# Ternary network of a two-layer kernel: VectorE normalises, copies and splits the next batch's rows two slots ahead of their old places

## The chip, the cores and the metric

One core of a Trainium2 chip runs the whole program. The time is device microseconds for one execution. Four compute engines work side by side, each with its own instruction stream, and wait for each other by semaphores: TensorE (PE: matmuls and transposes; its weight loads are PEld), VectorE (DVE), ScalarE (ACT) and GpSimd (POOL). SyncE (SP) issues the DMAs that store the result.

## The reference

The input is x, 16 batches of 512 rows of 256. Four parts are added to it in turn, each fed with a layer norm of x; only the last one is touched here:

```python
def _ternary_linear(x, w):
    alpha = jnp.mean(jnp.abs(w))
    w_t = jnp.sign(w) * (jnp.abs(w) > 0.5 * alpha).astype(w.dtype)
    ...
    rms = jnp.sqrt(jnp.sum(x * x, axis=-1, keepdims=True)) / jnp.sqrt(jnp.asarray(d, x.dtype))
    x_norm = x / (rms + EPS)
    return jnp.einsum('bsd,fd->bsf', x_norm, w_q)
h = jax.nn.gelu(_ternary_linear(x, w_up), approximate=False)
return _ternary_linear(h, w_down)
```

x has 256 columns, h has 1024. The weights become -1, 0 or 1; the rows are scaled by their root mean square before each of the two products. The second scale is applied at the end, to the finished product.

## The kernel before, in words

All 16 batches of x stay in SBUF. The last of the four parts is `ternary_feed_forward` (from L2180). It works one batch after the other (b = 0 to 15) and, in each, in eight slots (f = 0 to 7), one for each 128 of the 1024 hidden columns. A slot has the number n = 8b + f, so there are 128 slots. Each engine has its own hand-written loop over n, and the order of calls in a loop is the order of that engine's work.

What one slot does:

- **TensorE** (`up`, L2221, matmuls at L2230): four matmuls of 128 x 512 make the hidden columns in one of three PSUM banks. Four, because x is kept as two float32r parts, a rounded one and the rest, and has two halves of 128 columns.
- **ScalarE**: `gelu` (L2275) in place in the bank, `high_part` (L2280), the rounded copy of h, and `square` (L2292).
- **VectorE**: `low_part` (L2326), the rest of h, which is h less its rounded copy.
- **GpSimd** (L2406): adds the squares up over the eight slots of a batch, in slots 1 to 7.
- **TensorE** again, three slots later (`T_LAG`): `down` (L2234, matmuls at L2244), eight matmuls of 128 x 256 into the PSUM banks of the batch's result. In the loop of TensorE a slot is thus `up(n)`, then `down(n - 3)`.

Around it, once for each batch, stands the preparation of the next batch's rows, in two pairs of 128-row tiles:

- `normal(b + 1, pair)` (L2302, instructions at L2309) on VectorE writes two normalised tiles into `shared_xn`, a buffer for one pair.
- `turn_x(b + 1, pair)` (L2214, transposes by the helper `turn_blocks`, L120) on TensorE turns them into `prep_bank`, one PSUM bank that both pairs use in turn, after slot 1 (pair 0) and after slot 4 (pair 1). It waits for the normalised pair, and for `low_x` of the pair before, which has to have read the bank.
- `keep_x` (L2316) on VectorE copies the bank out as the rounded part, and `low_x` (L2320) writes the rest. Both read `prep_bank`, so `keep_x` waits for `turn_x` of its own pair.

The last part is the end of a batch. After slot 7 TensorE adds the squares over the partitions (`row_sums`, L2255, of the batch before). Then come `hidden_mean` on VectorE, `hidden_root` on GpSimd (L2395), and in slot 0 of the batch after that `hidden_scale` on VectorE (L2336, L2338). `finish(b - 2, t)` (L2344) multiplies a tile of the product out of PSUM by its scale and adds it to x: tiles 0 and 1 in slot 0, tiles 2 and 3 in slot 1 behind that slot's `low_part`. Two pairs of PSUM banks hold the products of the batches by turns, so the first `down` of batch b, which TensorE issues in slot 3, waits for the four `finish` of batch b - 2:

```python
q.wait_ge(s["x_added"], added(b - 2) if b >= 2 else 0)
```

The other wait of this kind is in `up(n)`: it needs `low_part(n - 3)`, which has to have read the PSUM bank. The order of VectorE's work is set by the constant at L2179: `T_XN_AT` says in which slots the two `normal` stand, `T_TURN_AT` where `turn_x` stands on TensorE, `T_KEEP_AT` where `keep_x` and `low_x` stand.

Of the kernel before, what the change touches and what calls it, by code (L numbers as in the profile page):

```python
# [1709 lines left out]
FC = F // P  # L1710
# [465 lines left out]
H_BANKS = 3  # L2176


T_XN_AT, T_TURN_AT, T_KEEP_AT, T_SUMS_AT = (0, 2), (1, 4), (2, 5), 7  # L2179
def ternary_feed_forward(net, ternary, start, result):  # L2180


# [1 line left out]
    nc, B, L, D, T = net.nc, net.B, net.L, net.D, net.T  # L2184
    n_slots = B * FC
    with ExitStack() as ctx:
# [112 lines left out]
        def dve(q):  # L2299
            e = q.e  # L2300

            def normal(b, pair):  # L2302
                late = b >= FIRST_ROWS
                q.wait_ge(s["scale"], 2 if late else 0)
                q.wait_ge(s["turned"], 2 * b + pair)
                for tt in range(2):
                    t = b * T + 2 * pair + tt
                    by = scale[:, t - start.rows:t - start.rows + 1] if late else start.scale[:, t:t + 1]
                    i = e.tensor_scalar(xn[:, tt, :], net.x[:, t, :], net.mean_var[:, t, 0:1], by,  # L2309
                                        ALU.subtract, ALU.mult)  # L2310
                i.then_inc(s["xn"])

            def keep_x(b, pair):
                q.wait_ge(s["turned"], 2 * b + pair + 1)
                q.wait_ge(s["up"], (b - 1) * FC)
                e.tensor_copy(x_part(b, pair, 0), prep_bank[:, :].rearrange("p (c t) -> p c t", c=2)).then_inc(s["x_hi"])  # L2316

            def low_x(b, pair):
                q.wait_ge(s["x_hi"], 2 * b + pair + 1)
                e.tensor_tensor(x_part(b, pair, 1), prep_bank[:, :].rearrange("p (c t) -> p c t", c=2), x_part(b, pair, 0),  # L2320
                                ALU.subtract).then_inc(s["x_lo"])

            def low_part(n):
                q.wait_ge(s["h_hi"], n + 1)
                q.wait_ge(s["h_squared"], n + 1)
                e.tensor_tensor(h_parts[:, n % H_BUFS, 1, :], h_banks[n % H_BANKS][:, :], h_parts[:, n % H_BUFS, 0, :],  # L2326
                                ALU.subtract).then_inc(s["h_lo"])

            def hidden_mean(b):
                q.wait_ge(s["h_rows"], b + 1)  # L2330
                e.tensor_scalar(hs[:, b % 2, :], prep_bank[:, 0:T], 1.0 / F, None, ALU.mult).then_inc(s["h_mean"])

            def hidden_scale(b):
                out = hs[:, b % 2, :]
                q.wait_ge(s["h_rms"], b + 1)
                e.tensor_scalar(out, out, 1e-8, None, ALU.add).then_inc(s["h_rms_eps"])  # L2336
                q.wait_ge(s["h_rms_eps"], b + 1)
                e.reciprocal(out, out).then_inc(s["h_scale"])  # L2338

            def finish(b, t):  # L2340
                xs = net.x[:, b * T + t, :]
                q.wait_ge(s["h_scale"], b + 1)
                q.wait_ge(s["down"], (b + 1) * FC)
                e.scalar_tensor_tensor(out=xs, in0=down_banks[2 * (b % 2) + t // 2][:, (t % 2) * D:(t % 2 + 1) * D],  # L2344
                                       scalar=hs[:, b % 2, t:t + 1], in1=xs, op0=ALU.mult, op1=ALU.add).then_inc(s["x_added"])

            def scales():
                q.wait_ge(s["std"], 2)
                e.reciprocal(scale[:, :], scale[:, :]).then_inc(s["scale"])
                q.wait_ge(s["scale"], 1)  # L2350
                e.tensor_tensor(rms[:, :], rms[:, :], scale[:, :], ALU.mult).then_inc(s["rms"])
                q.wait_ge(s["rms"], 1)
                e.tensor_scalar(rms[:, :], rms[:, :], 1e-8, None, ALU.add).then_inc(s["rms"])
                q.wait_ge(s["rms"], 2)
                e.reciprocal(rms[:, :], rms[:, :]).then_inc(s["rms"])
                q.wait_ge(s["rms"], 3)
                e.tensor_tensor(scale[:, :], scale[:, :], rms[:, :], ALU.mult).then_inc(s["scale"])

            for f in range(FC):
                e.tensor_copy(up_w[:, :, f * P:(f + 1) * P], ternary.up[:, :, f * P:(f + 1) * P]).then_inc(s["up_wide"])  # L2360
            for n in range(n_slots + 2 * FC):
                b, f = divmod(n, FC)
                if n < n_slots:
                    low_part(n)
                if b + 1 < B and f in T_XN_AT:
                    normal(b + 1, T_XN_AT.index(f))
                if b + 1 < B and f in T_KEEP_AT:
                    keep_x(b + 1, T_KEEP_AT.index(f))
                    low_x(b + 1, T_KEEP_AT.index(f))
                if 0 < b <= B and f == T_SUMS_AT:  # L2370
                    hidden_mean(b - 1)
                if n == SCALES_AT:
                    scales()
                if 2 <= b < B + 2 and f == 0:
                    hidden_scale(b - 2)
                if 2 <= b < B + 2 and f < 2:
                    finish(b - 2, 2 * f)
                    finish(b - 2, 2 * f + 1)
# [41 lines left out]
        with nc.Block() as block:  # L2420
            @block.sync
            def _(e):
                sp(Seq(e))

            @block.scalar
            def _(e):
                act(Seq(e))

            @block.vector
            def _(e):  # L2430
                dve(Seq(e))

            @block.gpsimd
            def _(e):
                pool(Seq(e))

            @block.tensor
            def _(e):
                pe(Seq(e))
# [47 lines left out]
```

## Time and profile before

| | us |
|---|---|
| median of 3 runs | 2664.49 (2663.3 to 2668.45) |
| the profiled execution | 2662.7 |
| its span in the profile | 2660.9 |
| ternary part in the profile, from its first matmul | 2363.5 to the end |
| mean granted share of the TensorE clock | 0.986 |

The profiled execution is 1.8 us longer than its span, since a little lies around the span, and it is 1.8 us below the median of the runs. In the profile "idle before" is time in which an engine did nothing just ahead of an instruction, with the engine and line that ended the wait. The full granted clock, 1.00, is 2.4 GHz; 0.50 is 1.2 GHz. A matmul's duration runs to its modelled end, which lies behind the start of the next.

### The profile page before, as it was taken

How to read it: one execution, taken by the hardware profiler on the slowest of the kernel's cores; microseconds unless marked ns; L12 is line 12 of the kernel's file. 1: busy time of each engine (PE TensorE's matmuls, PEld its weight loads, DVE VectorE, ACT ScalarE, POOL GpSimd, SP SyncE). 2: the span in 40 equal slices, each digit the busy share in tenths (PEclk: the TensorE clock that was granted, in tenths of full speed). 3: DMA queues.
4: the chain of work that ended last, by engine and by line, in shares of the span. 5: the costliest groups of instructions: out<-in, count | busy, mean ns of one | idle time of the engine just before them, and what ended most of it. 6: DMA issues, size and time to landing. Idle time of an engine off the chain costs nothing. (4 is left out here: it accounts for less than half of the span.)

```text
span 2660.9 us, 73392 instructions
## 1 busy us (share of the span) xinstructions
PE 2514.8 (95%) x26276; PEld 1807.2 (68%) x26276; DVE 2135.9 (80%) x6793; ACT 2003.7 (75%) x3679; POOL 1693.0 (64%) x3088
## 2 busy tenths in 40 slices
PE   5999999999999999999879999999999999989998
PEld 3677777777777777777523336777777776768887
DVE  5999999999989999998674667888888888746665
ACT  4998999998899998998624447766676667657776
POOL 3767667667667767767451227777776777756555
PEclk8999999999999999999989999999999999999999
DMA  4334234334234434425100126566566556400001
GB/s 124 64 67 83 56 67 84 72 58 84 62 60 84 79 57 78 73 48 86 36 8 1 36 51 115 96 104 106 93 102 104 103 97 98 71 2 25 33 33 40
DMA packets 110378, 182.09 MB, mean 68 GB/s; under 512 B 27008, under 2 KB 96384, under 8 KB 97920
## 3 DMA queue, kind: packets, MB, share of 16 engines
q1 hardware_dynamic: 106176, 175.82, 35.5%
q8 instruction: 211, 3.46, 0.6%
q10 hardware_dynamic: 3840, 1.58, 0.3%
q14 instruction: 151, 1.24, 0.2%
HBM read 116.25 MB, written 60.29 MB: 66 GB/s over the span
## 5 line engine op out<-in xcount | busy, mean ns | idle before, releaser
L923 POOL TENSOR_TENSOR ratio_scores<-ratio_scores,ratio_max_cols 128x512 f32<-128x512 f32 (+3 forms) x1024 | 727.7, 728 | 318.3 <-DVE ratio_max_cols L808 312.5
L199 PE MATMUL bank<-ratio_k_stack,ratio_q_stack 102*128 102x512 bf16 (+7 forms) x2048 | 506.0, 303 | 33.6 <-DVE ratio_max_cols L808 17.5
L1483 DVE CUSTOM_DVE_ANT_0 zeroed_unused<-bank,zeroed_drop 128x512 bf16<-128x512 f32 (+3 forms) x1024 | 439.7, 484 | 107.3 <-PE bank L199 107.2
L808 DVE CUSTOM_DVE_ANT_0 ratio_scores<-bank,ratio_scores 128x512 f32<-128x512 f32 (+3 forms) x1024 | 472.5, 490 | 22.2
L1365 ACT ACTIVATE arena<-bank 128x512 f32<-128x512 f32 x640 | 370.3, 593 | 150.8 <-PE bank L1258 149.4
L657 ACT ACTIVATE ratio_prob<-bank 128x512 f32<-128x512 f32 x640 | 378.7, 592 | 104.9 <-PE bank L555 102.4
L798 DVE TENSOR_TENSOR ratio_scores<-bank,ratio_inverse 128x512 f32<-128x512 f32 x640 | 436.2, 682 | 16.8 <-PE bank L199 9.6
L552 PE MATMUL bank<-const_f_sb,ratio_scores 128*128 128x128 f32 x2560 | 410.0, 274 | 0.9 <-ACT ratio_prob L657 0.9
L646 ACT ACTIVATE ratio_inverse<-bank 128x512 f32<-128x512 f32 x640 | 381.1, 596 | 12.5 <-PE bank L202 12.5
L650 ACT ACTIVATE ratio_inverse<-ratio_inverse 128x1024 f32<-128x1024 f32 x320 | 338.7, 1058 | 10.1
L1617 POOL TENSOR_SCALAR_AFFINE_SELECT arena<-arena 128x256 f32<-128x256 f32 (+1 forms) x640 | 229.1, 364 | 163.7 <-ACT arena L1365 159.8
L552 PEld LDWEIGHTS bank<-const_f_sb,ratio_scores 128*128 128x128 f32 x2560 | 301.5, 141 | 42.3 <-issue 2.0
L199 PEld LDWEIGHTS bank<-ratio_k_stack,ratio_q_stack 96*128 96x128 bf16 (+1 forms) x2048 | 179.0, 98 | 193.4 <-DVE ratio_max_cols L808 109.3
L1258 PE MATMUL bank<-zeroed_q_stack,zeroed_k_stack 99*128 99x128 bf16 x2560 | 249.7, 219 | 11.7 <-ACT arena L1365 10.6
L199 PE MATMUL bank<-zeroed_k_stack,zeroed_q_stack 96*128 96x512 bf16 (+3 forms) x1024 | 248.0, 305 | 2.8 <-PEq L2153 2.1
L1258 PEld LDWEIGHTS bank<-zeroed_q_stack,zeroed_k_stack 99*128 99x128 bf16 x2560 | 178.2, 97 | 91.5 <-ACT arena L1365 55.5
L2406 POOL TENSOR_TENSOR ternary_square_sum<-ternary_square_sum,ternary_squares 128x512 f32<-128x512 f32 x112 | 144.8, 1293 | 121.3 <-ACT ternary_squares L2292 120.9
L555 PE MATMUL bank<-const_b_sb 128*128 128x128 bf16 x1024 | 211.9, 219 | 0.0
L202 PE MATMUL bank<-const_b_sb 128*128 128x128 bf16 x1024 | 193.1, 220 | 0.0
L1951 ACT ACTIVATE lowrank_hidden<-bank,lowrank_b 128x512 f32<-128x512 f32 x128 | 82.2, 684 | 133.5 <-PE bank L1833 133.4
L214 PE MATMUL bank<-arena,zeroed_v_ones 128*32 128x128 f32 x5120 | 179.4, 276 | 0.9
L214 PE MATMUL bank<-ratio_prob,ratio_v_ones 128*32 128x128 f32 x5120 | 179.4, 276 | 0.0
(219 smaller groups left out, 4973.6 us busy)
## 6 DMA issues: line engine op xcount, KB each, us to landing
ratio_q_stack<-ratio_parts_q SPq DMA_DIRECT2D x186, 128.0 KB
ratio_k_stack<-ratio_parts_k SPq DMA_DIRECT2D x186, 128.0 KB
zeroed_q_stack<-zeroed_parts_q SPq DMA_DIRECT2D x186, 128.0 KB, 4.4
zeroed_k_stack<-zeroed_parts_k SPq DMA_DIRECT2D x186, 128.0 KB, 7.5
ratio_parts_q<-arena SPq DMA_DIRECT2D x96, 128.0 KB
ratio_parts_k<-arena SPq DMA_DIRECT2D x96, 128.0 KB
zeroed_parts_q<-shared_parts SPq DMA_DIRECT2D x96, 128.0 KB
zeroed_parts_k<-shared_parts SPq DMA_DIRECT2D x96, 128.0 KB
```

The costliest lines, as they stand in the source:

```text
L199: i = e.matmul(bank[:, off:off + w], qs[0:rows, s, hh, ib * P:(ib + 1) * P], ks[0:rows, s, hh, 0:w], start=(k == 0), stop=mask is None, sk ...
L214: i = e.matmul(o_bank[32 * h:32 * h + 32, ib * P:(ib + 1) * P], values_ones[:, vs, jb, (g % 2) * GROUP + h, :], prob[:, (base + u) % bufs, ...
L552: e.matmul(bank[:, at], scores[:, n % S_BUFS, at], net.ident, is_transpose=True, start=first, stop=False, skip_group_check=True)
L646: e.activation(inv[:, n % INV_BUFS, :], shared("denoms", n)[:, :], ACT.Ln, scale=-2.0, bias=EPS_RATIO).then_inc(s["log_den"])
L650: e.activation(both, both, ACT.Exp, scale=-1.0).then_inc(s["inverse"])
L657: e.activation(prob[:, n % PROB_BUFS, 0:wd], exp_banks[n % 2][:, 0:wd], ACT.Exp).then_inc(s["prob"])
L798: e.tensor_tensor(scores[:, n % S_BUFS, 0:wd], dot_banks[n % 2][:, 0:wd], inv[:, n % INV_BUFS, 0:wd], ALU.mult).then_inc(s["weighed"])
L808: i = e.tensor_tensor_reduce(seg, dot_banks[n % 2][:, at], seg, 1.0, 0.0, ALU.mult, ALU.max, mx[:, pair % M_BUFS, c:c + 1])
L923: i = e.tensor_tensor(seg, seg, mx[:, pair % M_BUFS, c:c + 1].to_broadcast([P, w]), ALU.subtract)
L1258: i = e.matmul(bank[:, off + jb * P:off + (jb + 1) * P], ks[0:STACK + FOLD_ROWS, st, hh, jb * P:(jb + 1) * P], qs[0:STACK + FOLD_ROWS, st, ...
L1365: e.activation(prob[:, n % FOLD_PROBS, 0:wd], exp_banks[n % 2][:, 0:wd], ACT.Exp, scale=0.25).then_inc(s["prob"])
L1483: i = e.tensor_tensor_reduce(unused[:, n % 2, at], bank[:, at], drop[:, L - (ib + 1) * P:L], 1.0, 0.0, ALU.add, ALU.max, mx[:, pair % FOLD ...
```

## The change

Three constants and VectorE's loop change. TensorE's loop stays as it is, with its transposes after slots 1 and 4.

```diff
-T_XN_AT, T_TURN_AT, T_KEEP_AT, T_SUMS_AT = (0, 2), (1, 4), (2, 5), 7
+T_XN_AT, T_TURN_AT, T_KEEP_AT, T_SUMS_AT = (-2, 0), (1, 4), (0, 3), 7
...
             for f in range(FC):
                 e.tensor_copy(up_w[:, :, f * P:(f + 1) * P], ternary.up[:, :, f * P:(f + 1) * P]).then_inc(s["up_wide"])
+            normal(1, 0)
             for n in range(n_slots + 2 * FC):
                 b, f = divmod(n, FC)
                 if n < n_slots:
                     low_part(n)
-                if b + 1 < B and f in T_XN_AT:
-                    normal(b + 1, T_XN_AT.index(f))
                 if b + 1 < B and f in T_KEEP_AT:
                     keep_x(b + 1, T_KEEP_AT.index(f))
                     low_x(b + 1, T_KEEP_AT.index(f))
+                if b + 1 < B and f == T_XN_AT[1]:
+                    normal(b + 1, 1)
+                if b + 2 < B and f == FC + T_XN_AT[0]:
+                    normal(b + 2, 0)
                 if 0 < b <= B and f == T_SUMS_AT:
                     hidden_mean(b - 1)
```

VectorE's order in one batch, by slot, each time behind that slot's `low_part`:

| slot | before | after |
|---|---|---|
| 0 | normal pair 0; hidden_scale; finish 0, 1 | keep_x, low_x pair 0; normal pair 1; hidden_scale; finish 0, 1 |
| 1 | finish 2, 3 | finish 2, 3 |
| 2 | normal pair 1; keep_x, low_x pair 0 | |
| 3 | | keep_x, low_x pair 1 |
| 5 | keep_x, low_x pair 1 | |
| 6 | | normal pair 0 of the batch after the next |
| 7 | hidden_mean | hidden_mean |

## Rows read from the trace of the kernel before

**Rows 1.** The page: busy time of each engine, its share of the span.

```profile
PE 2514.8 (95%) x26276; PEld 1807.2 (68%) x26276; DVE 2135.9 (80%) x6793; ACT 2003.7 (75%) x3679; POOL 1693.0 (64%) x3088
```

**Rows 2.** Busy time by stretch: stretch, length, five engines, clock, DMA share, GB/s.

```profile
2380.00:2655.00 275.00, 262.48 (x1718) 235.88 (x1716) 172.18 (x347) 202.81 (x365) 158.74 (x127) 1.00 0.08 28
```

**Rows 3.** Who waited for whom, TensorE, ternary part: us in total, times, longest.

```profile
PE bank L120 <- DVE shared_xn L2309: 7.5, 15, 1.8
PE bank L120 <- DVE ternary_x_parts L2320: 2.9, 7, 1.0
PE bank L120 <- DVE ternary_first_parts L2320: 2.5, 7, 0.4
```

**Rows 4.** Timeline of TensorE, batch 5, slots 1 to 4: start, us, what.

```profile
2457.15 1.11 PE L2244 MATMUL bank<-ternary_down_wide,ternary_h_parts 128*128 128x256 f32 x8
2458.67 0.66 PE L120 MATMUL bank<-const_f_sb,shared_xn 128*128 128x128 f32 x4 [0.41 <-DVE shared_xn L2309]
2459.08 1.17 PE L2230 MATMUL bank<-ternary_x_parts,ternary_up_wide 128*128 128x512 f32 x4
...
2461.04 1.09 PE L2230 MATMUL bank<-ternary_x_parts,ternary_up_wide 128*128 128x512 f32 x4
2461.97 1.11 PE L2244 MATMUL bank<-ternary_down_wide,ternary_h_parts 128*128 128x256 f32 x8
...
2465.30 0.63 PE L120 MATMUL bank<-const_f_sb,shared_xn 128*128 128x128 f32 x4 [0.35 <-DVE ternary_first_parts L2320]
```

**Rows 5.** Timeline of VectorE, batch 5, slots 0 to 3.

```profile
2457.89 0.73 DVE L2309 TENSOR_SCALAR shared_xn<-x,mean_var,ternary_first_scale 128x256 f32<-128x256 f32 x2
...
2459.74 0.68 DVE L2326 TENSOR_TENSOR ternary_h_parts<-bank,ternary_h_parts 128x512 fp32r<-128x512 f32 x1
2460.33 0.87 DVE L2344 SCALAR_TENSOR_TENSOR x<-bank,ternary_h_scale,x 128x256 f32<-128x256 f32 x2
...
2462.70 1.14 DVE L2309 TENSOR_SCALAR shared_xn<-x,mean_var,ternary_first_scale 128x256 f32<-128x256 f32 x2
2463.75 0.68 DVE L2316 CAST ternary_first_parts<-bank 128x512 fp32r<-128x512 f32 x1
2464.47 0.69 DVE L2320 TENSOR_TENSOR ternary_first_parts<-bank,ternary_first_parts 128x512 fp32r<-128x512 f32 x1
2465.07 1.46 DVE L2326 TENSOR_TENSOR ternary_h_parts<-bank,ternary_h_parts 128x512 fp32r<-128x512 f32 x2
```

**Rows 6.** Timeline of GpSimd, batch 5, slots 1 and 2.

```profile
2459.13 1.30 POOL L2406 TENSOR_TENSOR ternary_square_sum<-ternary_square_sum,ternary_squares 128x512 f32<-128x512 f32 x1 [2.38 <-ACT ternary_squares L2292]
2462.06 1.29 POOL L2406 TENSOR_TENSOR ternary_square_sum<-ternary_square_sum,ternary_squares 128x512 f32<-128x512 f32 x1 [1.64 <-ACT ternary_squares L2292]
```

**Rows 7.** Timeline of TensorE, batch 0, slots 1 to 3.

```profile
2368.82 0.66 PE L120 MATMUL bank<-const_f_sb,shared_xn 128*128 128x128 f32 x4 [1.81 <-DVE shared_xn L2309]
...
2370.50 1.91 PE L2230 MATMUL bank<-ternary_first_parts,ternary_up_wide 128*128 128x512 f32 x4
2372.20 0.41 PE L2244 MATMUL bank<-ternary_down_wide,ternary_h_parts 128*128 128x256 f32 x1
```

**Rows 8.** Timeline of TensorE: behind a short wait and behind two long ones.

```profile
57.60 0.39 PE L199 MATMUL bank<-ratio_k_stack,ratio_q_stack 96*128 96x256 bf16 x2 [1.29 <-DVE ratio_max_cols L808]
...
1314.13 0.70 PE L1833 MATMUL bank<-arena 64*128 64x512 f32 x2 [2.13 <-PEq L1007]
...
2324.60 0.23 PE L1266 MATMUL bank<-const_b_sb,zeroed_m_parts 128*128 128x128 bf16 x1 [1.83 <-POOL zeroed_m_parts L1609]
```

**Rows 9.** Busy time by stretch: after three long waits of TensorE, and around a short one.

```profile
1315.22:1318.63 3.41, 3.39 (x12) 1.11 (x10) 1.17 (x3) 3.27 (x5) 0.06 (x1) 0.50 0.71 211
...
2325.56:2328.97 3.41, 3.17 (x19) 2.67 (x17) 2.86 (x12) 1.61 (x6) 3.08 (x12) 0.50 0.02 4
2369.94:2373.35 3.41, 3.41 (x13) 2.83 (x12) 0.81 (x2) 2.54 (x5) 1.20 (x2) 0.50 0.00 0
57.00:62.50 5.50, 4.68 (x42) 4.01 (x43) 5.40 (x18) 4.13 (x7) 4.31 (x7) 1.00 1.09 170
```

## The prediction, made before the changed kernel was run

> **What bounds the kernel now.** I read the page first: TensorE is busy for 95% of the span [rows 1]. The change touches only the ternary part, so I then read the busy time by stretch for it: from 2380 to 2655 us TensorE is busy for 262.5 of 275 us at the full clock, while VectorE has 172 us of work [rows 2]. TensorE bounds this part, and a change pays or costs by what it does to TensorE's waits. The view of waits names them: 7.5 us before transposes for `normal`, and 2.9 + 2.5 us before transposes for `low_x`, 12.9 us in all, over 15 batches that prepare a next one [rows 3]. These are the waits the change moves work away from. VectorE has room on average, so the question is only which of its results comes late inside a batch.
>
> The timelines of batch 5 give the steady pattern. Every batch's `down` in slot 1 is followed by a wait of 0.41 us, then the transposes; those of pair 1 wait 0.35 us [rows 4]. A matmul group's modelled end lies 0.16 us behind the next group's start where nothing waits (2461.04 + 1.09 against 2461.97 [rows 4]), and this overlap is lost at a wait. So the two waits cost 0.57 + 0.51 = 1.08 us per batch.
>
> **What is removed.** After the change `normal` of pair 0 is made in slot 6 of the batch before, and `low_x` of pair 0 ends in slot 0 or 1, long before TensorE reaches slot 4. Both waits go: 1.08 us in each of batches 1 to 14. No instruction is added or removed, and no DMA is issued elsewhere in the order, except that the store of a batch's result waits for `finish`; it is off the path until the last batches, where the order is unchanged.
>
> **What is added.** `keep_x` of pair 0 now stands in slot 0 of VectorE and waits for transposes that TensorE issues at the end of slot 1. Behind it in VectorE's queue stand `low_x`, `normal` of pair 1, `hidden_scale`, `finish` 0 and 1, `low_part` of slot 1 and `finish` 2 and 3. For the last two somebody waits: the first `down` of the batch, in slot 3, needs all four `finish`. I walk through batch 5, with slots 0 to 3 as n = 40 to 43.
>
> 1. TensorE, nothing waited for: `down(38)` starts at 2457.15 and the transposes follow 0.94 later (the spacing of 2461.04 to 2461.97), at 2458.09; today 2458.67 [rows 4]. Everything behind moves up by 0.58 as well: `down(40)` could start at 2461.39 in place of 2461.97.
> 2. The transposes take 0.63 [rows 4]; VectorE starts some 0.04 later, at 2458.76 (I estimate this handover from the 0.05 between the end of `normal`, 2458.62, and the transposes, 2458.67 [rows 4, 5]).
> 3. `keep_x` to `low_x` is 0.72, `low_x` to the next instruction 0.60 [rows 5]: `normal` of pair 1 starts at 2460.08.
> 4. GpSimd's addition of slot 1 runs from 2459.13 to 2460.43 [rows 6]. Today the pair that starts at 2462.70 beside the addition of 2462.06 to 2463.35 takes 1.14 us and ends 0.49 behind it; with GpSimd idle a pair takes 0.73 [rows 5, 6]. So I let the pair end at 2460.43 + 0.49 = 2460.92, not at 2460.81.
> 5. From the end of the pair of `normal` to the start of `low_part` is 1.12 (2458.62 to 2459.74, with `hidden_scale` and `finish` 0 and 1 between); from there to `finish` 2 and 3 is 0.59, and these take 0.87 [rows 5]. They end at 2463.50. TensorE can start `down(40)` at 2463.55.
>
> That is 2.16 us after 2461.39, of which about 2.0 will show as idle time. Of the 2.16 us, 1.08 is paid for by the two waits removed: **net +1.08 us per batch**. It falls on the batches that both prepare a next one and finish an old one, b = 2 to 14, 13 batches: +14.0 us. The bounds of the stall: without the GpSimd collision and with immediate handovers it is 2.0; with a whole addition of 1.30 waited for [rows 6] in place of 0.11 it is 3.3. I take 2.16, as the addition's end is known from the same timeline.
>
> `up(44)` in slot 4 needs `low_part(41)`, which ends at 2462.7 in this walk, before `down(40)`; so this does not add a second wait. `low_part` of slot 4 comes some 1.5 us later than today and nobody needs it before slot 7. In slot 6 `normal` stands where VectorE waits for ScalarE anyway.
>
> **Step 4 by rule.** The trace shows the longer pair beside GpSimd's addition [rows 5, 6]. The Trainium skill, page "SBUF — State Buffer", section "SBUF: two separate sides", says that VectorE and GpSimd share one pair of ports as an exclusive lock and that the one that starts first holds it for the whole instruction. By that rule the pair waits for the addition's end, as in step 4; without it the 13 stalls would sum to 1.4 us less.
>
> **The first batches.** Batch 1 has no `finish` in it and only gains, 1.1 us. Batch 0 waits 1.81 us today before its first transposes, and later runs at half clock: `up(3)` to `down(0)` takes 1.70 us there (2370.50 to 2372.20) [rows 7], against 0.93. With `normal(1, 0)` ahead of the loop the wait of 1.81 + 0.16 = 1.97 us can go, and the half-clock stretch of 2369.94 to 2373.35 [rows 9] with it (1.53 us, worked out below): 3.5 us at most. But `low_part(1)`, which `up(4)` needs, then stands behind `keep_x`, `low_x` and the pair of `normal`, 0.72 + 0.60 + 1.14 = 2.5 us of work [rows 5], of which some 1 us will show. I take 2.3 us, between 0.5 (the half-clock stretch stays and the 1 us shows) and 3.5. Sum so far: 14.0 - 1.1 - 2.3 = **+10.6 us**.
>
> **The clock.** New waits of 2.0 us are as long as those behind which the clock fell. The waits that ended at 1314.13 (2.13 us), at 2324.60 (1.83 us) and at 2368.82 (1.81 us) [rows 7, 8] were each followed, some 1 us after their end, by a stretch of 3.41 us at 1.2 GHz [rows 9]; behind a wait of 1.29 us, which ended at 57.60 [rows 8], the clock stayed at 2.4 GHz [rows 9]. In such a stretch two groups of 1.70 us find room that take 0.94 each at full clock: 3.41 - 1.88 = 1.53 us lost. If all 13 stalls are followed by one: 13 x 1.53 = **+19.9 us**. The likeliest sum is 10.6 + 19.9 = +30.5 us. Against the profiled execution's 2662.7 that is 2693.2; the median of the runs shown lies 1.8 higher, so I forecast 2695.
>
> The Trainium skill speaks against this term: the page "TensorE: Matmul & The Clock Gate", section "HAM oscillation — how this bites in real kernels", warns only of idle gaps longer than any in this walk. By that page the clock would stay up. The rows speak the other way, three of three, but it is a rival below.
>
> **Rivals.**
> - *The stall comes and the clock holds.* For it: each wait stands alone in a batch of otherwise unbroken matmuls. Against: the wait of 1.83 us had matmuls on both sides too. The time is 2664.5 + 10.6 = 2675. A mix is possible: with 8 of 13 stalls followed by a slow stretch it is 2687.
> - *Faster.* The place is `down` of slot 3 and its wait for `finish` 2 and 3. If VectorE had them done by 2461.39 in batch 5's terms, nothing would be late and each batch would gain its 1.08: 14 x 1.08 + 2.3 = 17.4 us less, 2647. It decides at a stall of 1.08 us; above that the batch loses. My chain ends 2.16 late, and every link of it is a row, so the chain would have to be a whole microsecond shorter. That could be only if `keep_x` were not held by the transposes; but it reads what they write.
> - *No change in effect:* the removed waits come back as waits of about 1.1 us, for `finish` or for `low_part`, 2664 give or take 4. This needs a chain 1.1 us shorter, too.
>
> **Chances.** Stall with most stalls followed by slow clock (2685 to 2702): 0.66. Stall without, or with few: 0.24. Faster: 0.05. Even: 0.05. A measurement of this kernel can tell about 0.2%, 5.3 us, from no change; both stall cases lie above it. The range of 8 in 10 reaches from the clock-holding case, 2674, to the forecast plus a stall 0.5 us longer in 13 batches, 2702. All in all faster 0.05, same 0.05, slower 0.90.
>
> **What would show it.** In the waits of the changed kernel the transposes' waits for L2309 and L2320 should be gone but for batch 0, and a new line should stand there: TensorE, L2244, waiting for `finish` (L2344), 13 times, some 26 us in total, 2.0 each. VectorE should show some 1 us idle before `keep_x` of pair 0, released by the transposes. Of the clock, stretches of 3.4 us at 0.50 should follow the stalls, and the distance from batch to batch should grow by 1.1 us without and by 2.6 us with one. The forecast is wrong if the new wait is under 1.1 us or absent, or if the granted clock stays at 1.00 throughout.

## The result, and the profile after

The changed kernel takes 2694.77 us (median of 6 runs, 2687.2 to 2698.14) against 2665.69 for the kernel before in as many runs. The ratio is 1.0102 with a 95% interval of 1.0083 to 1.0121: slower by 29 us. The forecast was 2695, range 2674 to 2702.

The view of waits, TensorE, ternary part of the changed kernel (us in total, times, longest), against [rows 3]:

```profile
PE bank L2244 <- DVE x L2344: 27.5, 13, 2.1
PE bank L120 <- DVE shared_xn L2309: 1.4, 1, 1.4
```

The 29 waits of the transposes, 12.9 us in all, are gone but for the first one. In their place stand 13 waits of the first `down` of a batch for `finish`. To see why that wait is 2.1 us long, read VectorE's timeline of batch 5 from the top, slots 0 to 2 (compare [rows 5]):

```profile
2456.14 0.69 DVE L2326 TENSOR_TENSOR ternary_h_parts<-bank,ternary_h_parts 128x512 fp32r<-128x512 f32 x1 [2.02 <-ACT ternary_square_sum L2292]
2457.59 0.69 DVE L2316 CAST ternary_first_parts<-bank 128x512 fp32r<-128x512 f32 x1 [0.76 <-PE bank L120]
2458.32 0.69 DVE L2320 TENSOR_TENSOR ternary_first_parts<-bank,ternary_first_parts 128x512 fp32r<-128x512 f32 x1
2458.93 0.83 DVE L2309 TENSOR_SCALAR shared_xn<-x,mean_var,ternary_first_scale 128x256 f32<-128x256 f32 x2
...
2460.87 0.68 DVE L2326 TENSOR_TENSOR ternary_h_parts<-bank,ternary_h_parts 128x512 fp32r<-128x512 f32 x1
2461.47 0.87 DVE L2344 SCALAR_TENSOR_TENSOR x<-bank,ternary_h_scale,x 128x256 f32<-128x256 f32 x2
```

and TensorE's of the same stretch (compare [rows 4]):

```profile
2456.01 1.11 PE L2244 MATMUL bank<-ternary_down_wide,ternary_h_parts 128*128 128x256 f32 x8
2456.95 0.60 PE L120 MATMUL bank<-const_f_sb,shared_xn 128*128 128x128 f32 x4
2457.31 1.17 PE L2230 MATMUL bank<-ternary_x_parts,ternary_up_wide 128*128 128x512 f32 x4
2458.31 1.10 PE L2244 MATMUL bank<-ternary_down_wide,ternary_h_parts 128*128 128x256 f32 x8
2459.25 1.09 PE L2230 MATMUL bank<-ternary_x_parts,ternary_up_wide 128*128 128x512 f32 x4
2462.48 1.88 PE L2244 MATMUL bank<-ternary_down_wide,ternary_h_parts 128*128 128x256 f32 x8 [2.14 <-DVE x L2344]
2464.16 1.91 PE L2230 MATMUL bank<-ternary_x_parts,ternary_up_wide 128*128 128x512 f32 x4
```

The transposes follow the `down` 0.94 us later and wait for nothing. VectorE stands idle 0.76 us before `keep_x`, and the two last `finish` end at 2462.34. TensorE starts `down` at 2462.48, 2.14 us idle. What follows is the second half of the loss: this `down` takes 1.68 us to the start of the next `up` and not 1.02, as the one of 2524.41 does behind its wait, for the clock has fallen. Busy time by stretch, with the clock as the third number from the end, behind two of the waits and behind a third:

```profile
2421.70:2425.11 3.41, 3.41 (x14) 3.02 (x14) 0.45 (x1) 0.69 (x2) 0.35 (x1) 0.50 0.45 154
2442.18:2445.59 3.41, 3.41 (x14) 3.02 (x13) 0.64 (x2) 0.38 (x1) 0.56 (x1) 0.50 0.46 156
2524.41:2527.82 3.41, 3.41 (x25) 3.24 (x26) 1.05 (x2) 1.24 (x3) 0.98 (x1) 1.00 0.46 154
```

At 0.50 the same 3.41 us hold 14 matmuls, at 1.00 they hold 25. The DMA engines were as busy in the third as in the other two (0.46, 0.45, 0.46), so their traffic doesn't set the slow stretches apart. In the profiled execution 11 of the 13 waits were followed by one; the first, of 2.03 us, and the seventh, whose end is at 2524.41, were not. The price of one can be read from the starts of `low_part` of slot 0 in batches 8, 9 and 10:

```profile
2518.06 0.69 DVE L2326 TENSOR_TENSOR ternary_h_parts<-bank,ternary_h_parts 128x512 fp32r<-128x512 f32 x1 [2.00 <-ACT ternary_square_sum L2292]
...
2537.25 0.69 DVE L2326 TENSOR_TENSOR ternary_h_parts<-bank,ternary_h_parts 128x512 fp32r<-128x512 f32 x1 [2.02 <-ACT ternary_square_sum L2292]
...
2557.91 0.69 DVE L2326 TENSOR_TENSOR ternary_h_parts<-bank,ternary_h_parts 128x512 fp32r<-128x512 f32 x1 [2.00 <-ACT ternary_square_sum L2292]
```

Batch 8, with a wait and no slow stretch, is 19.19 us long; batch 9, with both, is 20.66. The kernel before needs 17.92 to 17.99.

The books of the two profiled executions: from the first `up` to the end of the span it was 297.4 us before (2363.5 to 2660.9) and is 324.7 now (2360.8 to 2685.5), +27.3. The whole spans differ by 24.6 only, because the work ahead of the ternary part, the same in both, happened to end 2.7 us earlier (in the twelve profiles of this document the first `up` starts anywhere from 2359.9 to 2366.3). This profiled execution is among the quick ones of its kernel (2687.2, the others 2688.61 to 2698.14), so it has less than the whole 29 us in it.

### The profile page after: what moved, and what is told of

It is laid out like the page before. It is cut to its first block and busy times, and to the rows that moved or that the text cites. A ratio compares the mean times of both kernels' runs of the same rounds, so it can differ in the third digit from the quotient of the medians.

```text
span 2685.5 us, 73406 instructions
## 1 busy us (share of the span) xinstructions
PE 2522.7 (94%) x26276; PEld 1815.8 (68%) x26276; DVE 2137.3 (80%) x6793; ACT 2003.5 (75%) x3679; POOL 1688.2 (63%) x3088
## 3 DMA queue, kind: packets, MB, share of 16 engines
q10 hardware_dynamic: 3840, 1.58, 0.4%
```

## Experiments

All times are medians, and each is compared with the kernel before on the same chip in the same hours, whose median was 2662.96, 2664.7 and 2666.53 us in the three sets. In the first set are the finish first, eight matmuls in the wait, `normal` behind and `normal` only; in the last one matmul in the wait and GpSimd's wait; the rest in the second. The sets ran on different chips, and the changed kernel (2694.77 against 2665.69) belongs to none of them. So a difference between kernels of two sets is known only to some 3 us.

### The finish first

```diff
-T_XN_AT, T_TURN_AT, T_KEEP_AT, T_SUMS_AT = (-2, 0), (1, 4), (0, 3), 7
+T_XN_AT, T_TURN_AT, T_KEEP_AT, T_SUMS_AT = (-2, 1), (1, 4), (1, 3), 7
...
                 if 2 <= b < B + 2 and f < 2:
                     finish(b - 2, 2 * f)
                     finish(b - 2, 2 * f + 1)
+                if b + 1 < B and f == T_KEEP_AT[0]:
+                    keep_x(b + 1, 0)
+                    low_x(b + 1, 0)
+                    normal(b + 1, 1)
```

> The changed kernel, but keep_x and low_x of pair 0 and normal of pair 1 stand in slot 1 behind finish 2 and 3, not in slot 0 ahead of them. Theory (the four finish are late for the first down of a batch, and the clock falls behind each such wait): the wait of L2244 for L2344 is gone, no slow stretch is left in the ternary part, the waits of the transposes stay gone, and the time is some 17 us below the kernel before, 2648 to 2650 by its median of 2665.7. Rival one (making keep_x wait for transposes on VectorE is itself what costs): a wait of TensorE for low_part or for normal takes the place, time at 2665 or above. Rival two (the slower clock has another cause in this part): slow stretches remain, time 2655 to 2668.

Measured: 2645.8 us, ratio 0.993 (0.9917 to 0.9942). Behind the first matmuls of the ternary part the view of waits has one line for TensorE, and the clock holds over the steady batches (busy time by stretch):

```profile
PE bank L120 <- DVE shared_xn L2309: 0.2, 1, 0.2
```

```profile
2400.00:2640.00 240.00, 234.51 (x1566) 214.75 (x1564) 169.20 (x327) 184.07 (x331) 144.22 (x115) 1.00 0.10 35
```

The timelines of TensorE and VectorE in one batch show what is different:

```profile
2467.33 0.60 PE L120 MATMUL bank<-const_f_sb,shared_xn 128*128 128x128 f32 x4
...
2470.59 1.12 PE L2244 MATMUL bank<-ternary_down_wide,ternary_h_parts 128*128 128x256 f32 x8
```

```profile
2467.52 0.87 DVE L2344 SCALAR_TENSOR_TENSOR x<-bank,ternary_h_scale,x 128x256 f32<-128x256 f32 x2
2468.38 0.69 DVE L2326 TENSOR_TENSOR ternary_h_parts<-bank,ternary_h_parts 128x512 fp32r<-128x512 f32 x1
2468.99 0.87 DVE L2344 SCALAR_TENSOR_TENSOR x<-bank,ternary_h_scale,x 128x256 f32<-128x256 f32 x2
2469.77 0.68 DVE L2316 CAST ternary_x_parts<-bank 128x512 fp32r<-128x512 f32 x1
2470.49 0.69 DVE L2320 TENSOR_TENSOR ternary_x_parts<-bank,ternary_x_parts 128x512 fp32r<-128x512 f32 x1
```

VectorE does not stand idle for the transposes, which end at 2467.93: it starts the first `finish` at 2467.52 and has the last done at 2469.86, 0.73 us before the first `down` of the batch starts at 2470.59. `keep_x` then finds its bank full and does not wait. So neither the copies nor their being early cost anything; their place ahead of `finish` did. This version is 17 us faster than the kernel before. It is 49 us faster than the changed kernel by the medians, and 46 if each is taken against its own kernel before. Rival one and rival two of the expectation are out.

### Work in the wait

Eight matmuls of 128x512 that nobody needs, ahead of the first `down` of batches 2 to 14 of the changed kernel:

```diff
+            def fill(b):
+                q.wait_ge(s["x_lo"], 2 * (b + 1) + 1)
+                for k in range(FILL):
+                    e.matmul(prep_bank[:, :], up_w[:, 0, 0:P], x_parts[b % 2][:, 0, 0, :], start=True, stop=True)
...
                 if n < n_slots:
                     up(n)
+                if 2 <= b < B - 1 and f == T_LAG:
+                    fill(b)
```

> The changed kernel with 8 more matmuls of 128x512 on TensorE ahead of the first down of batches 2 to 14, written to the bank of the transposes, where nobody reads them: work added into the wait for finish, about 1.8 us of it. Theory (the wait costs its net 1.1 us and, apart from that, the clock that falls behind it costs 1.5 us each): the wait shrinks to about 0.3 us, the start of the down stays where it was, the slow stretches are gone, and the kernel with 104 more matmuls is faster than the changed one by 11 to 13 times 1.53 us: about 2676. Rival (the slow stretches are no effect of the wait, or such matmuls don't count as work for the clock): time unchanged, 2692 to 2697, with slow stretches as before.

Measured: 2673.89 us, ratio 1.0038 (1.0023 to 1.0053). The kernel does 104 matmuls more than the changed one and is 21 us faster by the medians, 18 if each is taken against its own kernel before. Timeline of TensorE, and the clock over the steady batches:

```profile
2457.04 1.98 PE L2263 MATMUL bank<-ternary_x_parts,ternary_up_wide 128*128 128x512 f32 x8
2459.32 1.19 PE L2245 MATMUL bank<-ternary_down_wide,ternary_h_parts 128*128 128x256 f32 x8 [0.30 <-DVE x L2352]
```

```profile
2400.00:2640.00 240.00, 236.49 (x1503) 210.59 (x1502) 146.78 (x292) 166.91 (x301) 126.67 (x102) 1.00 0.09 30
```

The `down` still comes late (`finish` sets its start), but the clock holds. This separates the two halves: 10.9 us above the kernel before (2673.89 less 2662.96; 6 to 14 by the interval) for the lateness alone, the rest of the 29 us for the clock. The batches say the same: they are 19.12 to 19.18 us long here, and 19.19 in the changed kernel where no slow stretch fell into one. The `down` is as late as before and only the idle time ahead of it is filled, so the idle time is what brought the clock down.

### A control for the added matmuls

The same eight matmuls in the version with the finish first, behind the first `down` (same `fill`, the call two lines lower).

> Control: the kernel with the copies behind the finish (which has no wait left) with the same 8 matmuls in the same slot of the same 13 batches, behind the first down. Theory (in the changed kernel they were hidden in the wait): here nothing hides them and each batch is 1.8 to 2.0 us longer: 2645.8 + 25 = 2671, between 2668 and 2673. Rival (such matmuls cost little anywhere): under 2655.

Measured: 2667.67 us, which is 21.9 us above 2645.8, 1.68 for each batch, just under the expected range; in the profiles the batches are 18.6 us long against 16.8, 1.8 more. Eight matmuls do cost time where no wait hides them. That they cost nothing, and less than nothing, in the changed kernel is due to the wait.

### Most of the wait left idle, and nearly all of it

`FILL = 2` and `FILL = 1` in place of 8, in the changed kernel.

> As the kernel with 8 added matmuls ahead of the first down, but 2 of them: the idle wait is then 1.7 us, the down starts at the same time. Theory (what the clock costs hangs on how much of the wait is idle): few slow stretches, as behind the 1.6 us waits of the kernel with normal behind the finish, 2673 to 2680. Rival (any wait of 1.5 us or more in this pattern brings the clock down, or the 8 matmuls helped for another reason than idle time): slow stretches behind most waits, 2688 to 2697.

> As the kernels with 8 and with 2 added matmuls ahead of the first down, with one: idle waits of 1.9 us, between the 1.7 us behind which the clock never fell and the 2.12 us behind which it fell 11 times of 13. Theory (idle time decides): some of the 13 waits are followed by a slow stretch, 3 to 10 of them, 2680 to 2691. Rival (a sharp length): none, 2675 to 2679, or as many as in the changed kernel, 2691 to 2697.

Measured: 2676.67 us with two (ratio 1.0039, 1.0020 to 1.0058) and 2694.62 with one (1.0114, 1.0093 to 1.0135). One matmul of some 0.2 us, 13 times, makes 18 us of difference (16 if each is taken against its own kernel before). The waits and the clock, with two matmuls:

```profile
PE bank L2245 <- DVE x L2352: 21.4, 13, 1.7
```

```profile
2400.00:2650.00 250.00, 228.60 (x1488) 205.01 (x1487) 152.78 (x306) 174.49 (x314) 133.29 (x106) 1.00 0.09 28
```

and with one:

```profile
PE bank L2245 <- DVE x L2352: 24.5, 13, 1.9
```

```profile
2400.00:2650.00 250.00, 225.54 (x1384) 201.77 (x1383) 146.83 (x294) 163.96 (x295) 126.54 (x101) 0.94 0.08 27
```

With waits of 21.4 / 13 = 1.65 us (the longest 1.68) none was followed by a slow stretch. With 24.5 / 13 = 1.88 us ten of 13 were; the three that were not had lasted 1.79, 1.89 and 1.90 us, and the shortest that was, 1.86. I had expected 2680 to 2691 with one matmul; it came out above, as slow as the changed kernel. In this kernel's pattern the step lies between 1.68 and 1.86 us, and a wait above it is followed by a slow stretch mostly, not always.

### The second pair of normal behind the finish

```diff
-T_XN_AT, T_TURN_AT, T_KEEP_AT, T_SUMS_AT = (-2, 0), (1, 4), (0, 3), 7
+T_XN_AT, T_TURN_AT, T_KEEP_AT, T_SUMS_AT = (-2, 1), (1, 4), (0, 3), 7
...
                     finish(b - 2, 2 * f + 1)
+                if b + 1 < B and f == T_XN_AT[1]:
+                    normal(b + 1, 1)
```

> The changed kernel, but normal of pair 1 stands in slot 1 behind finish 2 and 3; keep_x and low_x of pair 0 stay ahead of the finish. Theory: the chain to finish 3 is shorter by one pair of normal, 0.75 us, so the wait is 1.35 to 1.4 us in place of 2.12, the net loss per batch is 0.3 us, and at that length (behind 1.29 us the clock stayed up in the kernel before) no or few slow stretches follow: 2666 give or take 3. If the clock falls behind these waits too: 2680 to 2686. Rival (GpSimd's addition, beside which normal runs, sets the chain): the wait shrinks by less than 0.3 us.

Measured: 2667.1 us, ratio 1.0019 (1.0008 to 1.0029), clock 1.00 throughout the steady batches. The wait shrank to 1.6 us and not to 1.4:

```profile
PE bank L2244 <- DVE x L2344: 19.2, 12, 1.6
PE bank L2244 <- ACT ternary_h_parts L2280: 1.4, 1, 1.4
```

```profile
2457.11 0.38 DVE L2336 TENSOR_SCALAR ternary_h_scale<-ternary_h_scale 128x4 f32<-128x4 f32 x1
```

```profile
2456.17 1.29 POOL L2409 TENSOR_TENSOR ternary_square_sum<-ternary_square_sum,ternary_squares 128x512 f32<-128x512 f32 x1 [2.39 <-ACT ternary_squares L2292]
```

The last two fences explain the missing 0.2 us. The first instruction of `hidden_scale`, which takes 0.16 us elsewhere, now starts beside GpSimd's addition, takes 0.38 and ends at 2457.49, 0.03 behind the addition. Half a microsecond off the chain was worth 28 us by the medians (25 if each is taken against its own kernel before). 13 x 0.52 = 7 us of it is the shorter wait; the other three quarters came through the clock: 2.1 us waits became 1.6 us waits, below the step.

### Each part alone

First `normal` of pair 0 early, the copies in their old places; then the copies early, `normal` in its old places.

```diff
-T_XN_AT, T_TURN_AT, T_KEEP_AT, T_SUMS_AT = (0, 2), (1, 4), (2, 5), 7
+T_XN_AT, T_TURN_AT, T_KEEP_AT, T_SUMS_AT = (-2, 2), (1, 4), (2, 5), 7
...
+            normal(1, 0)
             for n in range(n_slots + 2 * FC):
...
+                if b + 2 < B and f == FC + T_XN_AT[0]:
+                    normal(b + 2, 0)
```

```diff
-T_XN_AT, T_TURN_AT, T_KEEP_AT, T_SUMS_AT = (0, 2), (1, 4), (2, 5), 7
+T_XN_AT, T_TURN_AT, T_KEEP_AT, T_SUMS_AT = (0, 2), (1, 4), (0, 3), 7
```

> The kernel before with one part of the change alone: normal of pair 0 in slot 6 of the batch before, and normal(1, 0) ahead of the loop; all else, keep_x and low_x too, in its old place. Theory: the 0.41 us wait of the transposes of pair 0 goes, 0.57 us with the lost overlap, in batches 1 to 14, and 2 to 3.5 us in batch 0; the waits of pair 1 stay: 8 to 11 us, 2655 to 2658. Rival (removed waits come back at the next wait, for low_x of pair 1): 2663 to 2666.

> The kernel before with the other part of the change alone: keep_x and low_x in slots 0 and 3, both normal in their old slots 0 and 2. Theory (chain of VectorE to finish 3): the transposes of pair 0 still wait 0.41 us for normal; the chain behind them has no normal of pair 1 in it, so the first down comes 1.4 to 1.5 us late, some 1.3 us idle; the wait of pair 1 goes. Net 0.9 to 1.0 us in 13 batches, no slow clock behind waits of 1.3 us: 2662.9 + 12 = 2675, between 2671 and 2679. Rival (it is the pair of normal in slot 0, beside GpSimd's addition, that delays, not the copies): 2663 to 2667.

Measured: 2656.94 us with the early `normal` alone, ratio 0.9973 (0.9962 to 0.9984), 6 us faster; 2676.9 with the early copies alone, ratio 1.0039 (1.0020 to 1.0058), 12 us slower. The waits of the first:

```profile
PE bank L120 <- DVE ternary_x_parts L2320: 4.8, 8, 1.6
PE bank L120 <- DVE ternary_first_parts L2320: 2.5, 7, 0.4
```

The early `normal` is the good half: the waits for it are gone and those for `low_x` stay. One of them is new, 1.29 us in batch 0: part of what that batch saved before its first transposes is paid again before its second. The longest, 1.58 us, lies in batch 2, where the kernel before waited 0.96. The waits of the second:

```profile
PE bank L2244 <- ACT ternary_h_parts L2280: 17.8, 13, 1.4
PE bank L120 <- DVE shared_xn L2309: 7.4, 15, 1.6
```

There the view names ScalarE for the 13 waits of `down`, 1.37 us each. It names the releaser it takes for the last. In batch 5 the two last `finish` end at 2466.35 and the `down` starts at 2466.50, 0.15 us later, as in the changed kernel (0.14). The `high_part` that ScalarE ended at 2466.38 is that of slot 3, and the `down` uses the one of slot 0. So I read them as the same wait. The parts alone add up to +6 us, together they make +29: the `normal` of pair 1 stands in the chain of `finish` only when both are moved, and that takes the wait over the step at which the clock falls. Behind the 13 waits of 1.37 us here it never did.

### The transposes a slot earlier, and GpSimd out of the way

If `keep_x` is held by transposes in slot 1, one could move those as well:

```diff
-T_XN_AT, T_TURN_AT, T_KEEP_AT, T_SUMS_AT = (-2, 0), (1, 4), (0, 3), 7
+T_XN_AT, T_TURN_AT, T_KEEP_AT, T_SUMS_AT = (-2, 0), (0, 3), (0, 3), 7
```

> The changed kernel with TensorE's transposes moved too, from slots 1 and 4 to slots 0 and 3, so that keep_x need not wait for them. Theory: VectorE's chain starts 0.9 us earlier, right behind low_part of slot 0. If normal of pair 1 then starts ahead of GpSimd's addition of slot 1, the wait of the first down shrinks from 2.1 to about 1.1 us, no slow stretches, 2660 to 2666. Rival (the shared port): normal still waits for the end of GpSimd's addition of slot 1, the chain ends where it did, the wait stays 1.6 to 2.1 us, and the time is 2675 to 2695.

Measured: 2692.74 us (4 runs), ratio 1.0100 (1.0059 to 1.0141): nothing gained, the theory's number was wrong and the rival's right. The wait of `down` is no shorter:

```profile
PE bank L2244 <- DVE x L2344: 28.1, 13, 2.5
```

One of these 13 waits is 1.12 us long, the others 2.19 to 2.54, and 9 of those 12 were followed by a slow stretch. VectorE and GpSimd in slot 0 of batch 5, in this kernel:

```profile
2461.97 1.79 DVE L2309 TENSOR_SCALAR shared_xn<-x,mean_var,ternary_first_scale 128x256 f32<-128x256 f32 x2
```

```profile
2462.31 1.29 POOL L2409 TENSOR_TENSOR ternary_square_sum<-ternary_square_sum,ternary_squares 128x512 f32<-128x512 f32 x1 [2.82 <-ACT ternary_squares L2292]
```

The copies no longer wait, but the pair of `normal` takes 1.79 us in place of 0.73: its first instruction got in ahead of the addition, the second ended 0.16 us behind the addition's end, 2463.60. To test that reading, GpSimd's addition of slot 1 was made to wait for that pair:

```diff
                     q.wait_ge(s["h_squared"], n + 1)
+                    if f == 1 and b + 1 < B:
+                        q.wait_ge(s["xn"], 2 * (b + 1) + 2)
```

> The kernel with TensorE's transposes a slot earlier, in which GpSimd's addition of slot 1 now waits for normal of pair 1, so that the two never overlap (one wait on GpSimd, which stood idle 2.8 us there). Theory (the shared port is what kept that kernel's chain late): the pair of normal in slot 0 takes 0.73 us in place of 1.79, the first down waits about 1.4 us in place of 2.5, no slow stretches: 2663 to 2668 against 2692.7. Rival (normal was late for another reason): the pair still takes over 1.5 us, the wait stays over 2, time 2685 or more.

Measured: 2664.17 us, 28.6 us less than without that wait by the medians (30 if each is taken against its own kernel before); level with the kernel before (0.9998, 0.9987 to 1.0010).

```profile
2455.13 0.73 DVE L2309 TENSOR_SCALAR shared_xn<-x,mean_var,ternary_first_scale 128x256 f32<-128x256 f32 x2
```

```profile
2456.00 2.71 POOL L2411 TENSOR_TENSOR ternary_square_sum<-ternary_square_sum,ternary_squares 128x512 f32<-128x512 f32 x2 [3.34 <-DVE shared_xn L2309]
```

```profile
PE bank L2244 <- DVE x L2344: 15.3, 13, 1.5
```

The pair is back at 0.73 us, the wait of `down` is 15.3 / 13 = 1.2 us, and the clock stays at 1.00 in the steady batches. An added wait made the kernel 28 to 30 us faster.

## Why the prediction was right, step by step

**The waits removed.** Right. Without any wait a batch takes 16.74 to 16.88 us in the version with the finish first, against 17.92 to 17.99: 1.1 us, the forecast's 1.08 in each of the batches.

**The chain of VectorE.** Right link by link. From `down` to transposes 0.94, foretold 0.94; transposes to `keep_x` 0.64 (0.67); to `low_x` 0.73 (0.72); to `normal` 0.61 (0.60); the pair 0.83 (0.84, with the collision); from its end to `low_part` 1.11 (1.12); to `finish` 0.60 (0.59); `finish` 0.87 (0.87). The one link mis-sized is the last handover, from `finish` to TensorE: 0.14 us where I took 0.05 from another pair of rows. The idle wait is thus 2.12 us (27.5 / 13) and not 2.0. The whole delay is 2.30 us where I had 2.16, since TensorE could have started its `down` 4.17 us behind `down(38)` (2460.18) and not 4.24.

**Which batches.** Right: 13 waits, b = 2 to 14. Net of the removed waits a batch without slow clock grew by 19.19 - 17.96 = 1.2 us (forecast 1.08), which is 2.30 less 1.08.

**The first batches.** Size off. From the first `up` to `low_part(8)` it was 2363.5 to 2384.80, 21.3 us, and is 2360.8 to 2378.92, 18.1 us: 3.2 us gained where I took 2.3 (bounds 0.5 and 3.5). The first transposes come 3.53 us behind the first `up`, not 5.30. That is 1.8 us gained of the 1.97 I allowed, though a wait of 1.41 us is left: `normal(1, 0)` stands behind the casts of the weights. Behind the transposes the half-clock stretch is gone. `low_part(1)` was late by less than I allowed: `up(4)` starts 1.20 us behind `down(0)` and not 0.94, so 0.26 us show and not 1. Batch 1 gained 1.2 (1.1). Part of this is the luck of one execution, for the clock of these first microseconds changes from profile to profile: 0.50 for the first 3 us and again later in the kernel before, 1.00 throughout in the changed one, 0.50 for 3 to 6 us in most of the others that have `normal(1, 0)` ahead of the loop.

**The clock.** Right in kind and price, 1.47 us for one (20.66 less 19.19; forecast 1.53), and nearly in number, 11 of 13 in the profiled execution. The sum for it: 13 x 1.2 less 3.2 less 1.2 is 11.2 us, with 11 x 1.5 = 16.5 it is 27.7, against 27.3 measured. The two halves were then measured apart: 10.9 us of lateness by the kernel with eight matmuls in the wait (forecast 10.6) and the rest, 18 us, by the clock (forecast 19.9; two of the 13 slow stretches that it counted didn't come). That the time itself, 2694.77, lies within 0.3 us of 2695 is luck: the increase was foretold as 30.5 us and is 29.1 by the medians, 27.3 in the ternary part of the profiles. Fewer and slightly cheaper slow stretches took away 3.7 us and the larger gain of the first batches 0.9; the longer waits gave 1.9 back. The page of the Trainium skill "TensorE: Matmul & The Clock Gate", section "HAM oscillation — how this bites in real kernels", warns of longer gaps only; here the trace differs, and waits of 1.9 to 2.1 us were followed by the slower clock in 10 and 11 of 13 cases.

**The shared port.** Right and small in the changed kernel (0.1 us), but large one move further: with the transposes earlier it was the term that kept the chain late. "SBUF — State Buffer", section "SBUF: two separate sides", of the Trainium skill, says this lock exists; the pair of 1.79 us beside GpSimd and 0.73 us without it agrees.

**The faster rival.** It missed the mark by the place of the work, not by its size: foretold 2647 if the chain were not late, and 2645.8 with the copies behind `finish`.

Open: why some of the waits of 2.1 us are spared a slow stretch (two of 13). The trace of the changed kernel shows an order in it. The slow stretch began 0.6 us behind the end of the second wait, 0.4 behind the third, 0.2 behind the fourth, at the end of the fifth and 0.2 us before that of the sixth; the seventh had none, behind the eighth it began 1.0 us late, and from there it crept forward again. Where it begins thus shifts from batch to batch, and the spared wait stands where it had come to the front. No run here was made to test that. The runs of the changed kernel spread over 11 us, those of the kernel before over 12, so that spread is nothing that the change brought.

## What to carry to other kernels

When work is moved ahead in an engine's queue, write down what it waits for and who waits for each item behind it: here two copies that wait 0.76 us for transposes stood ahead of four small operations that free PSUM banks. Put what somebody waits for first and the prefetch behind it; that alone turned +29 us into -17. And price a wait of TensorE by its length as well as by its count: here waits of up to 1.68 us cost themselves, and of those of 1.86 us and more most cost another 1.5 us by the clock.

## What the runs showed of the hardware

- In a pattern of one wait per 18 to 21 us of otherwise unbroken matmuls, idle waits of 1.37, 1.6 and 1.65 us never brought TensorE to 1.2 GHz (0 of 13 each). Those of 1.9 us did 10 times and those of 2.12 us 11 times of 13, those of 2.2 us 9 times of 12. Each time it was for 3.4 us and cost about 1.5 us.
- Eight matmuls whose result is thrown away, put into each such wait, made the kernel 18 to 21 us faster: with them the granted clock stayed at 1.00 over the steady batches, without them it was down behind 11 of 13 waits.
- VectorE's `tensor_scalar` beside GpSimd's `tensor_tensor` waited for its end even when it is tiny: 128x4 took 0.38 us in place of 0.16 and ended 0.03 us behind the addition. A pair of 128x256, 0.73 us by itself, took 0.83 with 0.34 us of the addition left at its start, 1.14 with 0.65 left, and 1.79 where the addition began 0.34 us behind it.
